# At an image's first tile, a turn and a product with V run on TensorE ahead of the new image's scores

## The reference, cut to what matters

```python
h = x.reshape(B, GROUPS, C // GROUPS, N)          # B 4, C 128, N 1024, GROUPS 32
h = (h - mu) * rsqrt(var + EPS)                   # mean and variance of a group and image
h = h.reshape(B, C, N) * gamma + beta
q, k, v = split(w_qkv @ h + b_qkv)                # each (B, N, C) after the transpose
attn = softmax(q @ k^T / sqrt(C))                 # (B, N, N)
out = w_proj @ (attn @ v)^T + b_proj
return x + out
```

## Time and profile before

| | us |
|---|---|
| median of 3 runs | 129.63 |
| lowest and highest | 129.54, 129.87 |
| the profiled execution | 130.25 |
| its span in the profile | 128.5 |

### The profile page before, as it was taken

One profiled execution on the slowest core, in us unless ns is written; L12 is line 12 of the kernel. 1 busy time (PEld: TensorE's weight loads), 2 busy tenths in 40 slices (PEclk: granted clock), 3 DMA queues, 4 the chain that ended last, 5 costly groups with the idle time before them and its releaser, 6 DMA issues.

```text
span 128.5 us, 3152 instructions
## 1 busy us (share of the span) xinstructions
PE 115.6 (90%) x1185; PEld 81.9 (64%) x1185; DVE 95.9 (75%) x246; ACT 89.0 (69%) x122; POOL 83.3 (65%) x59
## 2 busy tenths in 40 slices
PE   0599996988998999999989999999899999998971
PEld 0373554555764677667656886676568876777960
DVE  3669789999756967998578677775877777777823
ACT  1304419999798687887776878878868788788300
POOL 6000003969999988899768897999665756876000
PEclk9999999999999999999999999999999999999998
DMA  3692000898998999999999999999999999999922
GB/s 97 168 351 120 0 3 0 150 105 159 189 183 162 192 185 123 252 191 187 112 260 188 191 141 239 185 134 176 231 186 134 207 230 140 196 209 206 82 87 82
DMA packets 67502, 20.65 MB, mean 161 GB/s; under 512 B 65184, under 2 KB 65952, under 8 KB 67488
## 3 DMA queue, kind: packets, MB, share of 16 engines
q1 hardware_dynamic: 66720, 20.19, 87.0%
q10 hardware_dynamic: 704, 0.26, 0.8%
q0 software_dynamic: 64, 0.00, 0.0%
HBM read 2.36 MB, written 2.10 MB: 35 GB/s over the span
## 4 chain that ended last, share of the span: by engine, by line
POOL 52%; issue 20%; PE 10%; DMA 7%; ACT 4%; DVE 2%; POOLq 2%; ACTq 0%; SPq 0%
POOL p_hl L299 41%; POOL z_lo L292 5%; DMA ptT<-p_hl 4%; POOL z L279 3%; DMA wqkv_sb<-in_L_conv_w_qkv_dram 3%; PE scores L731 2%; ACT probs L358 2%; POOL z_hi L286 2%; POOLq L44 2%; ACT p_hl L365 2%; POOL rstd L271 1%; DVE row_max L455 1%; PE o_ps L690 1%; PE misc L640 1%; PE scores L710 1%
## 5 line engine op out<-in xcount | busy, mean ns | idle before, releaser
L299 POOL TENSOR_TENSOR p_hl<-probs,p_hl 128x1024 f16<-128x1024 f32 x31 | 65.9, 2130 | 26.4 <-ACT p_hl L365 26.1
L455 DVE TENSOR_REDUCE row_max<-scores 128x1 f32<-128x1024 f32 x32 | 39.1, 1221 | 19.3 <-PE scores L666 19.1
L358 ACT ACTIVATE probs<-scores,exp_bias,esc 128x1024 f32<-128x1024 f32 x32 | 38.5, 1203 | 18.8 <-DVE exp_bias L458 18.8
L365 ACT ACTIVATE p_hl<-probs 128x1024 f16<-128x1024 f32 x32 | 33.8, 1057 | 1.0
L682 PE MATMUL o_ps<-v_hi,ptT 128*128 128x128 f16 x256 | 32.0, 219 | 0.9 <-DMA ptT<-p_hl 0.5
L683 PE MATMUL o_ps<-v_lo,ptT 128*128 128x128 f16 x256 | 32.0, 219 | 0.0
L682 PEld LDWEIGHTS o_ps<-v_hi,ptT 128*128 128x128 f16 x256 | 25.0, 98 | 3.0 <-issue 0.8
L664 PE MATMUL scores<-z_hi,t_hi 128*128 128x512 f16 x64 | 24.3, 380 | 2.4 <-DVE t_lo L444 1.3
L683 PEld LDWEIGHTS o_ps<-v_lo,ptT 128*128 128x128 f16 x256 | 25.0, 98 | 0.2
L666 PE MATMUL scores<-z_hi,t_lo 128*128 128x512 f16 x64 | 24.3, 379 | 0.0
L665 PE MATMUL scores<-z_lo,t_hi 128*128 128x512 f16 x64 | 24.3, 379 | 0.0
(11 more groups left out here) (118 smaller groups left out, 138.6 us busy)
## 6 DMA issues: line engine op xcount, KB each, us to landing
out_dram<-out_sb SPq DMA_DIRECT2D x7, 256.0 KB, 3.6
x_sb<-in_x_dram SPq DMA_DIRECT2D x3, 512.0 KB, 4.5
ptT<-p_hl SPq DMA_TRANSPOSE x61, 3.4
x_sb<-in_x_dram SPq DMA_DIRECT2D x2, 256.0 KB, 3.3
out_dram<-out_sb SPq DMA_DIRECT2D x1, 192.0 KB, 2.0
wqkv_sb<-in_L_conv_w_qkv_dram ACTq DMA_DIRECT2D x1, 128.0 KB, 4.0
wqkv_sb<-in_L_conv_w_qkv_dram ACTq DMA_DIRECT2D x1, 64.0 KB, 3.7
wp_sb<-in_L_conv_w_proj_dram ACTq DMA_DIRECT2D x1, 64.0 KB, 3.8
```

The lines of the kernel that those rows point to most:

```text
L299: nc.gpsimd.tensor_tensor(p_hl[:, g % RING, 1], probs[:, g % RING], p_hl[:, g % RING, 0], ALU.subtract).then_inc(plo_ready, 1)
L358: nc.scalar.activation(probs[:, g % RING], scores[:, g % SLOTS], ACT.Exp, bias=exp_bias[:, g:g + 1], scale=esc[:], accum_out=row_sum[:, g: ...
L365: nc.scalar.activation(p_hl[:, g % RING, 0], probs[:, g % RING], ACT.Copy).then_inc(phi_ready, 1)
L455: nc.vector.tensor_reduce(row_max[:, g:g + 1], scores[:, g % SLOTS], AX_X, ALU.max).then_inc(max_ready, 1)
```

## The change

Only the order of two engines' lists is changed, and only in the iterations where s is 0 and there are finished tiles, g = 8, 16 and 24. On PE, `score_tile(g)` moves behind `turn(g - 5)` and `values(g - 4)`. On VectorE, `add_input(g - 5)` moves ahead of `maxima(g)`; where it stayed, it would be behind an instruction that waits for scores that wait for later products. No instruction is added or taken away.

```diff
@@ -569,8 +569,11 @@   (VectorE)
                 done = g - LAG - 1
                 if done >= 0:
                     scale_output(done)
+
+                if s == 0 and done >= 0:
+                    add_input(done)
                 maxima(g)
-                if done >= 0:
+                if s > 0 and done >= 0:
                     add_input(done)
                 if g >= 1:
                     inverse_sum(g - 1)
@@ -744,13 +747,17 @@   (TensorE)
                 b, s = divmod(g, TILES)
                 if g == 1:
                     pe.wait_ge(wmat_ready, 1)
-                score_tile(g)
+
+                if s > 0 or b == 0:
+                    score_tile(g)
                 if g > LAG:
                     turn(g - LAG - 1)
                 if g >= LAG:
                     if g == LAG:
                         pe.wait_ge(vareps_ready, 2)
                     values(g - LAG)
+                if s == 0 and b >= 1:
+                    score_tile(g)
```

## The result

| | us |
|---|---|
| before, median | 129.62 |
| changed, median of 4 runs (133.88 to 134.69) | 134.61 |
| ratio, 95% interval | 1.0362, 1.0324 to 1.0400 |
| profiled execution of the changed kernel | 134.60 |
| its span | 132.8 |

The change makes the kernel 3.6% slower. 134.3 was forecast.

A forecast was written before the change was run, and what follows sets the result against it. PE was taken as the bound. Each of three boundaries would come 1.57 us later, 4.7 us in all on 129.63, giving 134.3 us; own range 133.6 to 135.3, and 132.8 to 135.5 for 8 times in 10.

The forecast's parts named there:

- What bounds the kernel: PE is what the others wait for, busy 17.57 of 17.70 us between boundaries; delays there are not won back.
- B: Rival: the shift is won back inside the image, leaving 3 x 0.32 = 1.0 us, 130.6; chance 0.06.
- C: Rival: GpSimd sets the pace and swallows PE's delays, 131.2, or 129.6 if all; chance 0.06.
- The first wait: PE before turn(3) at tile 8's boundary: idle 0.93 us instead of 0.61, since scale_output(3) stands behind t_low.
- The scores: Tile 8's scores start at 41.82 instead of 40.00, its maxima at 43.33 instead of 41.51: 1.82 us later.
- The second wait: PE before turn(4), behind tile 9's scores: idle 1.48 us instead of 0.28; the turn at 45.90 instead of 44.33.
- add_input: On VectorE, moved ahead of maxima beside an idle stretch: costs nothing, gains 0.25 us for what is behind.
- The sum: Three boundaries at 1.57 us each, 4.7 us later in all, for 134.3 us.
- Rival A: PE does turn and product while t_low runs; three waits of 0.61 us go, 127.8; chance 0.05.
- Rival D: PE's clock falls to half rate after boundary pauses, 3 x 2.6 = 7.7 us on top, 142.0; chance 0.03.

The follow-up runs named there:

- one_boundary: The changed kernel's two edits at g = 8 alone, g = 16 and 24 as in the kernel before; 131.24 us, ratio 1.0109.
- first_early: The changed kernel with VectorE's scale_output(g-5) moved ahead of t_low of the next image's first half; 132.59 us, ratio 1.0210.
- turn_only: The kernel before with only the turn ahead of the scores at g = 8, 16, 24; 131.16 us, ratio 1.0110.
- second_early: The changed kernel with scale_output(g-4) moved ahead of the boundary tile's maxima; median 132.61 us of 10 runs, ratio 1.0012 (two runs).
- add_stays: The changed kernel with add_input back behind the maxima at g = 8, 16, 24; 135.17 us, ratio 1.0408.
- both_early: The changed kernel with the scale_output edits of first_early and second_early together; median 130.02 us of 12 runs, ratio 0.9985 (six runs).
- second_early_act_store: second_early with the loop's six stores issued by ScalarE instead of SyncE; 131.53 us, ratio 1.0152.
- the control: The kernel before with the loop's six stores issued by ScalarE instead of SyncE; 129.88 us, ratio 1.0024.
- before_second_early: The kernel before with the next iteration's scale_output ahead of t_low of the second half in boundary iterations; 128.94 us, ratio 0.9946.
- first_two: both_early's order at g = 8 and 16, before_second_early's elsewhere; median 129.45 us of 7 runs, ratio 0.9949 (four runs).
- last_one: both_early's order at g = 24 alone, before_second_early's at the first two boundaries; median 131.09 us of 12 runs, ratio 0.9890 (three runs).
- t_low_first: before_second_early with t_low of the next image's first half right behind the last tile's maxima; median 128.17 us of 6, ratio 0.9856 (four runs).

## Why the prediction was right

- *What bounds the kernel.* Right. PE is busy 17.40 of 17.50 us between boundaries, one_boundary shows a shift that stays, and rivals B and C are out: the shift passes whole through every boundary and every image, and GpSimd's idle grew by 4.6 us (26.4 to 31.0), just what the boundaries cost.
- *The first wait.* Forecast 0.93, measured 0.92; first_early took 0.65 of it away and got 2.0 us back, turn_only made it alone and lost 1.3 (131.16 against 129.89 on its chip).
- *The scores.* Forecast 41.82, measured 41.79; maxima forecast 43.33, measured 43.29. Tile 4's low part was in time.
- *The second wait.* Forecast 1.48, the turn at 45.90; measured 1.47 and 45.86. second_early took it away at the boundary.
- *add_input.* The 0.25 shows as 0.26 in the brackets of add_stays.
- *The sum.* 3 x 1.57 = 4.7. At tile 30 ScalarE's exponential starts 4.64 later (118.36, before 113.72), the last turn 4.31 later (129.97, before 125.66). The 0.33 between was given back in the tail, where both kernels wait for tile 30's low part, the one before 0.78 us and the changed one 0.46. By medians it is 4.99, since the profiled run of before lay 0.63 above its median and that of the changed kernel at its own. No step up to the last tiles failed. What the prediction left out is that the tail gives 0.33 back; that the time by medians (134.61) still lies 0.3 above the forecast is within what the runs of one kernel differ by.
- *Rival A.* Its place was named rightly: it decides at scale_output(4). The way out that it names, `oT_sb` ready by 38.7, is none: PE has products for t until 39.39, and 39.39 + 1.50 is already past the 40.25 that it needs. What I did not see is that the other way, scale_output(4) ahead of the maxima, brings the gain up to turn(27) (both_early, 1.20 ahead) and that it would then be lost in the wait for tile 29.
- *Rival D.* The products behind the 1.47 us pause start at 46.02 and 46.08, 0.06 apart as elsewhere; the granted clock of the four runs is 0.999 to 1.000. The clock did not fall, and the Trainium skill's warning of half rate ("TensorE: Matmul & The Clock Gate", "HAM oscillation") did not come into play at pauses of this length. The stretch that this rival was priced by is at half rate by the spacing of its products; the granted clock of that stage reads 1.00:

```profile
10.00:12.00 2.00, 2.00 (x6) 0.75 (x5) 1.93 (x9) 1.31 (x3) 0.00 (x0) 1.00 0.33 135
```

Open: why some runs have a wait of 1 to 3 us for tile 29 and others next to none. The trace of second_early shows the transfers nearly stopping in the middle of it. From 108 to 122 us, 40 slices of 0.35 us:

```profile
GB/s 194 139 222 204 191 143 212 196 202 176 120 4 7 10 160 208 281 290 285 209 210 207 176 173 213 214 288 338 290 199 211 192 155 259 101 0 6 10 40 268
```

There are two stops of about 1.2 us, at 112 and at 120; the second falls between the issue at 116.86 and the landing at 121.9. Such stops stand in every trace, the kernel before's too. In the fourteen profiled runs the two things go together. Tile 29's high part took 3.2 to 3.8 us from issue to landing in eleven of them, and 4.5 to 5.0 in second_early, both_early and second_early_act_store, where a stop lies in between (120.2 to 121.5, 117.5 to 118.5, 119.5 to 120.9). In the control's run the stop, 119.2 to 120.6, lies in the transfer of the low part. No edit moved a stop, so that its place decides the wait is not shown.

The wait isn't all of it either. Of the runs of these variants 23 have a mean granted clock of 0.987 or less (once 0.974), among them every run above 130.8 of both_early, before_second_early, first_two and last_one, both long ones of t_low_first and the four longest of second_early. All others, and all of the kernel before, have 0.996 or more. A mean of 0.987 over 130 us is, as an estimate, 3.4 us at 1.2 instead of 2.4 GHz, which costs PE up to 1.7 us. That fits both_early, where the profiled run with its wait of 2.61 is at 129.81 and the runs at 0.987 lie from 131.09 to 131.92. None of these 23 has a trace, so whether the clock fell behind a wait at the end, or elsewhere and by itself, is open. In the profiled runs of second_early and both_early it stayed at 1.00 behind their pauses of 2.80 and 2.61 us.

## What to carry to other kernels

Before work is moved into a gap, compare when its own operands are ready with when the gap ends: here the result of the filler came 0.3 us after the gap was over. Then follow what the displaced work feeds: the engine that had to deliver the filler's next operand was itself in line behind the displaced scores, so the wait came back five times as long. The better way was on the engine that ends the gap: putting the awaited instruction ahead of two that PE needed only later took back 0.32 of the 0.61 us and displaced nothing on PE.

## What the runs showed that I had not expected

Taking PE's waits away did not give only shorter runs. Beside runs of 128 to 129 us stand runs of 131 to 132, 3 of 7 in first_two and 7 of 12 in last_one, while no run of the kernel before was above 130.43 and the changed kernel's four lie within 0.8. In the profiled runs a late transfer for tile 29 goes with the longer time, in the longest runs, which have no trace, the granted clock is lower, and which comes first is open. A queue of transfers that seems to keep up may do so only because the compute waits; that is my reading, not a result. And transfers nearly stop (under 30 GB/s, of some 200) for 0.8 to 1.6 us at a time, five to nine times between 36 and 121 us in each of the fourteen traces.
